# Masked blocks last in the value products, mu steps in pieces, later stores and reloads, and a fourth slab buffer in the first phase of an attention and mixture-of-experts kernel on 8 cores

## The reference, cut to what matters

```python
# per sequence x: [T=2048, C=2048]; 16 query heads of 128, 4 key/value heads
q, k, v = x @ wq, x @ wk, x @ wv;  q, k = rope(q), rope(k)
scores = q @ k.T / sqrt(128)
p_g = softmax(where(causal, scores, neg));  p_l = softmax(where(local, scores, neg))
x1 = layernorm(x + 0.5 * (p_g @ v + p_l @ v) @ wo)
# soft mixture of 16 experts with 128 slots each
x_ln = layernorm(x1) * gamma + beta
logits = l2norm(x_ln) * scale @ l2norm(mu, axis=0)      # mu: [2048, 16, 128]
dispatch = softmax(logits, axis=1);  combine = softmax(logits over all 2048 slots)
h = gelu(dispatch.T @ x_ln @ W1 + b1);  slot_out = h @ W2 + b2
out = layernorm(x1 + combine @ slot_out)
```

## Time and profile before

| what | value |
|---|---|
| three runs, us | 4929.79, 4594.17, 4884.55 (median 4884.55) |
| profiled execution, us | 4605.99 |
| its span on the slowest core (core 1), us | 4604.4 (the eight: 4560.2 to 4604.4) |
| mean granted TensorE clock, core 1 | 0.904 |
| busy share of the span | PE 77%, DVE 37%, ACT 26%, POOL 12% |
| first phase, us of the span | 0 to about 2810 |

### The profile page before, as it was taken

One profiled execution on the slowest core, in us unless ns is written; L12 is line 12 of the kernel. 1 busy time (PEld: TensorE's weight loads), 2 busy tenths in 40 slices (PEclk: granted clock), 3 DMA queues, 4 the chain that ended last, 5 costly groups with the idle time before them and its releaser, 6 DMA issues.

```text
span 4604.4 us, 66156 instructions; the slowest of 8 cores (4560.2 to 4604.4 us)
## 1 busy us (share of the span) xinstructions
PE 3542.8 (77%) x25120; PEld 2138.6 (46%) x25120; DVE 1696.5 (37%) x3526; ACT 1176.8 (26%) x1542; POOL 568.2 (12%) x1152
## 2 busy tenths in 40 slices
PE   5776676787785564575877777999979879999796
PEld 3333443544442332443544553567744335677442
DVE  2454454453442454444554443211113322111133
ACT  1122223344440111222434441221211122211111
POOL 1222122212110111111222210000000000000000
PEclk9888798999897787887999998999989989999998
DMA  9938455636527376265541133037774410467633
GB/s 186 201 104 153 102 129 106 115 115 104 110 78 131 101 142 125 88 119 117 121 100 42 47 105 129 33 124 247 243 264 183 154 72 37 144 237 248 228 137 128
DMA packets 131606, 615.71 MB, mean 134 GB/s; under 512 B 15328, under 2 KB 17376, under 8 KB 108768
## 3 DMA queue, kind: packets, MB, share of 16 engines
q1 hardware_dynamic: 106560, 430.06, 27.6%
q0 software_dynamic: 15520, 114.30, 18.8%
q10 hardware_dynamic: 9216, 67.11, 3.6%
HBM read 604.08 MB, written 188.74 MB: 172 GB/s over the span
## 4 chain that ended last, share of the span: by engine, by line
PE 53%; DMA 19%; DVE 9%; ACT 6%; issue 5%; POOL 5%; SPq 1%; another core or an unknown queue 1%; DVEq 0%; ACTq 0%; POOLq 0%
PE ob L964 10%; PE sc L882 10%; PE pr L344 7%; DMA AR<-wqkv_c 6%; PE pr L426 6%; PE ob L542 5%; DMA AR<-x1sp 3%; PE sc L509 3%; DMA out<-AR 2%; PE sc L1007 2%; ACT AR L513 2%; PE pr L372 2%; DMA AR<-wqkv_r 2%; POOL AR L525 1%; POOL AR L522 1%
## 5 line engine op out<-in xcount | busy, mean ns | idle before, releaser
L344 PE MATMUL pr<-AR 128*128 128x512 bf16 x2560 | 685.2, 406 | 202.0 <-DMA AR<-wqkv_c 103.8
L513 ACT ACTIVATE AR<-sc 128x1024 bf16<-128x1024 f32 (+2 forms) x640 | 565.6, 896 | 917.5 <-PE sc L509 908.9
L542 PE MATMUL ob<-AR 128*128 128x129 bf16 x4352 | 358.0, 231 | 320.4 <-POOL AR L529 245.6
L426 PE MATMUL pr<-AR 128*128 128x512 bf16 x2048 | 543.9, 399 | 52.7 <-DVE AR L434 30.5
L542 PEld LDWEIGHTS ob<-AR 128*128 128x128 bf16 x4352 | 298.6, 103 | 451.2 <-issue 407.1
L964 PE MATMUL ob<-AR 128*128 128x256 bf16 x4096 | 461.9, 273 | 0.0
L344 PEld LDWEIGHTS pr<-AR 128*128 128x128 bf16 x2560 | 246.8, 103 | 455.6 <-issue 276.2
L882 PE MATMUL sc<-AR 128*128 128x512 bf16 x2048 | 455.9, 381 | 0.2 <-issue 0.2
L964 PEld LDWEIGHTS ob<-AR 128*128 128x128 bf16 x4096 | 399.4, 98 | 57.5
L509 PE MATMUL sc<-AR 128*128 128x256 bf16 (+1 forms) x2304 | 350.0, 277 | 51.2 <-ACT AR L513 50.0
L509 PEld LDWEIGHTS sc<-AR 128*128 128x128 bf16 x2304 | 224.8, 102 | 180.9 <-issue 79.4
(11 more groups left out here) (97 smaller groups left out, 3910.5 us busy)
## 6 DMA issues: line engine op xcount, KB each, us to landing
AR<-w_c SPq DMA_DIRECT2D x256, 512.0 KB, 6.0
AR<-wqkv_c SPq DMA_DIRECT2D x168, 512.0 KB, 4.0
w_c<-W_r POOLq DMA_DIRECT2D x32, 2048.0 KB, 41.5
AR<-x SPq DMA_DIRECT2D x32, 1024.0 KB, 6.7
x1sp<-AR ACTq DMA_DIRECT2D x32, 1024.0 KB, 4.1
AR<-b SPq DMA_DIRECT2D x32, 1024.0 KB, 6.9
AR<-x1sp SPq DMA_DIRECT2D x32, 1024.0 KB, 5.6
out<-AR ACTq DMA_DIRECT2D x32, 1024.0 KB, 3.9
```

The source lines that it names most:

```text
L344: tm = p.pe(lambda e, b=b, c=c, w=w: e.matmul(out=pr[b], lhsT=w[:, c * 128:(c + 1) * 128], rhs=xT[:, c * 512:(c + 1) * 512], start=c == 0, ...
L426: tm = p.pe(lambda e, b=b, h=h, dg=dg, nt=nt, i=i: e.matmul(out=pr[b], lhsT=oT[i % 2][:, nt, h, :], rhs=wo[h][:, dg * 512:(dg + 1) * 512], ...
L513: ta = p.act(lambda e, b=b, eb=eb, lo=lo, hi=hi: e.activation(out=eb[:, lo:hi], in_=sc[b][:, 0:hi - lo], func=AF.Exp), tm, t_E_pe[h % 2])
L542: tm = p.pe(lambda e, q=q, o=o, j=j, eb=eb, kv=kv, last=last: e.matmul(out=ob[q][:, 0:129], lhsT=eb[:, o:o + 128], rhs=vaug[:, j, kv, 0:12 ...
```

## The change

- **Value products.** `pv(h, q)` now does only the blocks without a mask, each waiting for the chunk of exp that it reads. `pv_end(h, q)` does the masked block and the local sum. Its place for q = 0 is behind `pv(h, 1)`, for q = 1 behind the last scores of the next head. The four POOL steps become two of double size: the diagonal ones first, then the two copies. `turn` comes one head later.
- **`take_pr(hold=True)`**: an item of the projection keeps its PSUM tile, and what comes in between takes the other.
- **mu** is no generator any more: its pieces are emitted 1, 4, 5, 8, 9, 11, 15 and 20 ticks after its place; each half's sum has a PSUM tile of its own and is added on DVE. The places move to windows 1, 2, 3 and 8 to 11, each after every sixth item of the window.
- **Layer norm**: the pieces are emitted at 1, 2, 3, 13, 15, 20 and 30 ticks. `xl` lies in the lower half of the tile's own `y` buffer (two of them), so DVE's first step now waits for the store to `x1sp`, and the reload of `y` for the store to `xlnsp`.
- **Four slab buffers**, the fourth where `xlv` was; `load_slab(k + 4)`.
- **`precast`** is spread over its window; window 8 puts the eight output items of window 7 between its eight k and v items; in the other even windows k and v items stand between output items; `c_proj` is 1.5 times as large in window 15.

```diff
-        ring = [v(RING + i * 4096, BF16, 2048) for i in range(3)]
+        ring = [v(o, BF16, 2048) for o in (RING, RING + 4096, RING + 8192, XL)]
...
-        xlv = v(XL, BF16, 2048)
+        xlb = [v(Y + i * 8192, BF16, 2048) for i in range(2)]
...
+        def take_pr(hold=False):
+
+            i = 1 - prn[0]
+            if i == held[0]:
+                i = 1 - i
+            prn[0] = i
+            if hold:
+                assert held[0] is None
+                held[0] = i
             return i
...
+            def second():
+
                 tg = p.dve(lambda e: e.scalar_tensor_tensor(
-                    out=xlv, in0=y, scalar=rs[:, 1:2], in1=gamv, op0=ALU.mult, op1=ALU.mult),
-                    tx, t_gb[0], t_xl_st[0])
-                t_y_free[nt] = [tg, ts]
-                if i < 15:
-                    load_y(i + 1, nt)
+                    out=xl, in0=y, scalar=rs[:, 1:2], in1=gamv, op0=ALU.mult, op1=ALU.mult),
+                    t_norm[0], t_x1[el, n], t_gb[0])
+                tok["x"] = p.dve(lambda e: e.tensor_tensor(out=xl, in0=xl, in1=betv, op=ALU.add), tg)
...
+            for n_, fn in ((1, power), (2, bias), (3, apply), (13, second), (15, stats),
+                           (20, store), (30, reload)):
+                after(n_, fn)
...
+                    two = eb[:, jd * 256:jd * 256 + 384].rearrange("p (a c) -> p a c", a=3)[:, 0:3:2, :]
+                    tg = p.pool(lambda e, two=two: e.tensor_tensor(
+                        out=two, in0=two, in1=tri2, op=ALU.mult), ta)
                     if w > 0:
...
+                        o = (jd - 1) * 256
+                        two = eb[:, o:o + 512].rearrange("p (a c) -> p a c", a=4)[:, 0:4:3, :]
+                        tg = p.pool(lambda e, two=two, lc=loc[h % 2]: e.tensor_tensor(
+                            out=lc, in0=two, in1=tri2, op=ALU.mult), t_E_pe[h % 2])
+                    t_mask[h] = tg
...
+                for j in range(2 * w + q):
+                    o = j * 256 + 128 * q
+                    p.pe(lambda e, q=q, o=o, j=j, eb=eb, kv=kv: e.matmul(
+                        out=ob[q][:, 0:129], lhsT=eb[:, o:o + 128],
+                        rhs=vaug[:, j, kv, 0:129], start=j == 0, stop=False),
+                        t_ec[h, o // 1024], v_toks, ob_free[q], t_vone)
+
+            def pv_end(h, q):
...
                 if h > 0:
                     pv(h - 1, 1)
+                    pv_end(h - 1, 0)
                     yield c_p[1]
...
+                if h > 0:
+                    pv_end(h - 1, 1)
+                    yield 0.2
+                if h >= 4 and h % 2 == 0:
+                    turn((h - 4) // 2)
...
+            for n_, fn in ((1, lambda: square(0)), (4, lambda: add_up(0)), (5, lambda: square(1)),
+                           (8, lambda: add_up(1)), (9, root), (11, scale), (15, store),
+                           (20, more)):
+                after(n_, fn)
...
+                yield from out[0:2]
+                for n in range(2, 8):
+                    yield from out[n:n + 1]
+                    yield from kv[n - 2:n - 1]
+                yield from kv[6:]
...
+        MU_AT = {1: [0, 1, 2], 2: [3, 4], 3: [5, 6, 7], 8: [8], 9: [9, 10, 11], 10: [12, 13], 11: [14, 15]}
...
+                if pre and min(fa, fp) >= 1 - len(pre) / (len(pre_at[i]) + 0.5):
+                    precast(pre.pop(0))
```

More of the change, by code:

```diff
@@ L168, in build_program @@
               for i in range(2)]
-        loc = [[v(LOC + (i * 2 + j) * 256, BF16, 128) for j in range(2)] for i in range(2)]
+        loc = [v(LOC + i * 512, BF16, 256).rearrange("p (a c) -> p a c", a=2) for i in range(2)]
         gpv = [v(LOC + 1024 + i * 512, F32, 128) for i in range(2)]
@@ L378, in v_item @@
                     yield 1.05
[L379 to L380 removed]
+            t_ring_pe[k % 4] = tm
+            held[0] = None
+            load_slab(k + 4)
             t_xT_pe[0] = tm
@@ L422, in out_item @@
         def out_item(i, nt, dg):
-            b = take_pr()
+            b = take_pr(hold=True)
             tm = None
@@ L638, in mu_item, with square @@
         def mu_item(e_):
-            b = take_pr()
-            tm = None
-            ts = t_mu_in[e_]
-            for hf in range(2):
-                tq = p.dve(lambda e, hf=hf: e.tensor_tensor(
+            tok = {"tm": None}
+            def square(hf):
+                tok["q"] = p.dve(lambda e, hf=hf: e.tensor_tensor(
                     out=musq, in0=mus[:, hf * 1024:(hf + 1) * 1024],
-                    in1=mus[:, hf * 1024:(hf + 1) * 1024], op=ALU.mult), ts, tm)
+                    in1=mus[:, hf * 1024:(hf + 1) * 1024], op=ALU.mult), t_mu_in[e_], tok["tm"])
@@ L646, in mu_item, with add_up @@
+            def add_up(hf):
+                b = take_pr()
+                tm = None
                 for c in range(8):
-                    tm = p.pe(lambda e, b=b, c=c, hf=hf: e.matmul(
+                    tm = p.pe(lambda e, b=b, c=c: e.matmul(
                         out=pr[b][:, 0:128], lhsT=ones, rhs=musq[:, c * 128:(c + 1) * 128],
-                        start=hf == 0 and c == 0, stop=hf == 1 and c == 7),
-                        tq, pr_free[b], inc=c == 7)
-                yield 0.6
@@ L661, in mu_item @@
-            t_mu_st[0] = p.dma("sync", "D_must", d_muc[e_], mus, t)
-            t_mu_all[e_] = t_mu_st[0]
-            if e_ + 1 < NE and e_ != 3:
-                load_mu(e_ + 1)
-            yield 0.1
+                        start=c == 0, stop=c == 7), tok["q"], pr_free[b], inc=c == 7)
+                tok["tm"] = tm
+                if hf == 0:
+                    t = p.dve(lambda e, b=b: e.tensor_copy(out=muinv, in_=pr[b][:, 0:128]), tm)
+                    tok["s"] = t
+                else:
+                    t = p.dve(lambda e, b=b: e.tensor_tensor(out=muinv, in0=pr[b][:, 0:128],
+                                                             in1=muinv, op=ALU.add), tm, tok["s"])
+                    tok["s"] = t
@@ new lines, in store, with more @@
+            def store():
+                t_mu_st[0] = p.dma("sync", "D_must", d_muc[e_], mus, tok["s"])
+                t_mu_all[e_] = t_mu_st[0]
+                mu_left[0] -= 1
+            def more():
+                if e_ + 1 < NE and e_ != 7:
+                    load_mu(e_ + 1)
+            for n_, fn in ((1, lambda: square(0)), (4, lambda: add_up(0)), (5, lambda: square(1)),
+                           (8, lambda: add_up(1)), (9, root), (11, scale), (15, store),
+                           (20, more)):
+                after(n_, fn)
@@ L692, in items_of, with plain_items @@
         def items_of(i):
+            mus_ = [("m", e_) for e_ in MU_AT.get(i, [])]
+            for n, it in enumerate(plain_items(i)):
+                if mus_ and n and n % 6 == 0:
+                    yield mus_.pop(0)
+                yield it
+            assert not mus_
+        def plain_items(i):
             G = i // 2
@@ L779, in build_program @@
             n_it = len(list(items_of(i)))
-            c_proj = 4.2 * n_it
-            if i in MU_AT and MU_AT[i][0] in (0, 4):
+            c_proj = 4.2 * n_it * (1.5 if i == 15 else 1.0)
+            if i in MU_AT and MU_AT[i][0] in (0, 8):
                 load_mu(MU_AT[i][0])
-            for j in pre_at[i]:
-                precast(j)
+            pre = list(pre_at[i])
             if i == 8:
-                for it in [qk_item(4, s) for s in range(4)] + [v_item(4, kv) for kv in range(4)]:
+                first = [qk_item(4, s) for s in range(4)] + [v_item(4, kv) for kv in range(4)]
+                outs = [out_item(7, nt, dg) for nt in range(2) for dg in range(4)]
+                for it in [x for two in zip(first, outs) for x in two]:
                     for _ in it:
```

164 lines of the change are left out of this document (82 added, 82 removed).

## The result

The kernel is faster: 0.9216 of the time before (95% interval 0.9016 to 0.9415). The profiled execution took 4251.72 us where 4107 was forecast: the gain is 354 of the 499 us expected. (Executions in which one half of the chip was held at a lower clock are left out of every ratio; the highest times listed here are such ones.)

What follows compares the result with a forecast made beforehand. First phase bound by PE's queue standing still behind others. 4605.99 - 205 - 185 - 71 - 5 - 28 + 50 + 40 - 95 = 4107 us; own range 4000 to 4220 (chance 0.70), wider range 3960 to 4300.

Steps and rivals of the forecast that it cites:

- mu's squares: PE's waits at mu's sums for DVE's squares, first phase: 185 of 198.4 us gained, bounds 120 and 198.
- the DMA rival: DMA engines and DVE take back more than half of what slabs and masks give: 4315 us, chance 0.14.
- everything gained: Rival: the cover holds and the clock stays up, new waits at half price: 3910 us, chance 0.11.
- no change: Rival: masks' and mu's waits are replaced by waits of the same size: 4552 us, chance 0.03.
- slower: Rival: DVE's wait for x1sp's store becomes the first phase's clock: 5257 us, chance 0.02.
- the masks: PE's waits at the value products for POOL's masks: 205 of 245.6 us gained, 41 left, bounds 120 and 245.
- Clock: Matmuls at the low clock, first phase: less idle time gains 95 of 150 us, bounds 30 and 150.
- Denser queues: Shorter windows make DVE and ACT late more often in the first phase: 40 us added, bounds 0 and 130.
- the old stall: PE's longest wait at L575, from the old xlv store: 28 us gained, bounds 20 and 28.
- DVE's wait for x1sp: DVE newly waits for x1sp's store, some 90 us in all: 50 us added for PE, bounds 0 and 290.
- Slabs: PE's waits for weight slabs, first phase: 71 of 121.4 us gained, 50 left, bounds 20 and 115.
- Window 0: Bound by the DMA engines; the fourth buffer gains 5 of 60 us of waits, bounds 0 and 25.

Runs made afterwards that it cites:

- e10_late_musplit: Changed kernel with the layer norm's second part in single, later steps and mu's scaling in four steps; 4149.11 to 4164.20 us, ratio 0.9023 to the kernel before.
- e1: Changed kernel without DVE's addition of beta and three of four statistics steps of xl in each tile; 4153.26 to 4165.52 us, ratio 0.9014 to the kernel before.
- e6: Changed kernel with the layer norm's second part in single steps at separate ticks, same work; 4163.68 to 4175.64 us, ratio 0.9084 to the kernel before.
- e3: Changed kernel with three slab buffers and xl in a buffer of its own; 4225.53, 4229.06, 4242.25 us (one run 12573.78, unexplained), ratio 0.9179 to the kernel before.
- e2: Changed kernel with three slab buffers instead of four, nothing else different; 4273.43, 4291.14 and 4310.78 us, ratio 0.9301 to the kernel before.
- e7_burst: Changed kernel with the weight casts again in bursts at the start of each window; 4313.42, 4318.13, 4338.82 us, ratio 0.9418 to the kernel before.
- e12_changed_again: The changed kernel itself without any edit, a second series; 4235.71, 4247.08, 4248.53 and 4250.71 us, ratio 0.9221 to the kernel before.

## Why the prediction was right in direction and wrong in size

The direction and the place were right: one phase gets shorter, the waits for POOL and slabs go nearly and those for mu's squares mostly, DVE gets a new wait for x1sp, and the DMA rival (4315), everything gained (3910), no change (4552) and slower (5257) did not come true. The size was not: 4251.72 us, 145 above the 4107 and outside the forecast's own range of 4000 to 4220. By the forecast's own terms PE should have idled 877 - 205 - 185 - 71 - 5 - 28 + 50 + 40 = 473 us and lost 95 less to the clock. It idled 540, and its busy time fell by 5: 67 + 90 = 157, less the 12 us by which tail and second phase got shorter, 145.

**The step that failed: each wait was priced at what it lasts.** For the masks the 245.6 us became 16.2, better than "205 gained, 41 left". But the term took the gain in time to be the wait that goes, 205 us. Undone in the changed kernel the masks' part costs 50 us, done alone it gives 126. At the same matmul stands a second condition, `ob_free`, which the view did not show because it names the one that came last. The prediction asked whether exp would take the place; it never asked so of DVE, though `ob_free[q]` stands in the same call. What came there shows in both kernels: 55.3 us of waits for DVE before, 171.4 after, 186.1 with the masks' part alone.

**Clock: failed, 95 forecast, 5 measured** (3 as the mean of the eight cores). The granted clock rose from 0.87 to 0.90, not to the "0.93 or more" that was asked for, because slow time was cut out in which PE did nothing. The matmuls ran slow nearly as often as before. That the number of stops is what keeps them slow is tempting, and not shown: PE stopped 355 times before and 267 times after by the rows of its waits, but 267 times, too, in e10_late_musplit, where its busy time is 1811 us on the profiled core and 1844 as the mean of the eight, against 1863 and 1868.

**Denser queues: the sign right, the +40 too small.** PE's waits for DVE other than mu's squares rose by 150 us. With the terms that belong there, 50 for x1sp and -28 for the old stall, 62 were forecast, and that counts all of the 40 to DVE, though it was to hold waits for ACT too. The 88 us more are what e1 and e6 got back in part, by less in a row and by the same in smaller steps. The reason given ("60 to 70% load is more often late") was a reason of averages. The runs point to the stretch without a break, 6.3 us, against some 3 us until PE misses `ob`. Both numbers were in the prediction or before's trace.

**mu's squares: too much counted.** 185 of 198.4 were to go; 39.8 are left where "below 20" was asked for, so 159 went. Between square and sum lie three ticks, but the square itself stands in DVE's queue behind the same blocks, as at 352 us.

**DVE's wait for x1sp: right.** "Some 90 in all", 49.9 measured; worth 50 forecast, 56 to 60 by e3 against e2. Against the change the prediction held a rule of the Trainium skill (DMA: Bandwidth & Descriptors, Queues, rings and completion order: queues with work are served in turn), and read out of it that spreading the casts "only moves" the stretches in which others are slow. The trace agrees with the rule: a store is late beside a single cast too (20.3 us to landing at 1979 us, median 5.7, beside a cast issued at 1971 that landed after 24.9). It does not agree with what was read out of it: bursts give 136.5 us of such waits (e7_burst), spread casts 49.9. A cover of ten ticks takes up most of what one cast can do, and not what three do.

**Slabs: better than forecast**, 7.0 us left instead of 50 (15.1 in e12_changed_again). **Window 0**: no gain (5 forecast); PE's waits for cast slabs and xT are 38.3 and 32.3 against 39.8 and 20.5. **exp**: forecast to "rather grow", fell from 50.0 to 24.7; instead the projection waits 39.0 us for ACT's copy of `pr` (8.6 before). **Tail and second phase**: -10 and -2, within the bounds. **Window 15** took 114 us, as asked for.

In one sum: DVE's rows miss the forecast by 88 + 26 (mu) = 114. The others miss it by -25 (masks), -43 (slabs), -25 (exp, taken as unchanged), +15 (window 0) and +30 (ACT's copy), -48 in all; 114 - 48 is 66 of the 67 us by which the idle time missed.

Of the four signs by which the prediction said that it would be wrong (POOL at L581, exp over 100 us, DVE's wait for x1sp over 200, the second phase changed by over 20) none came: 16.2 us at L581, 24.7 for exp, 49.9 for x1sp, 2 us in the second phase. None of them looked at DVE and `ob`, where the miss was.

## What to carry to other kernels

Before you count a wait as gained, list every condition of the waiting instruction and ask when each of the others is met; where an in-order engine with half its time busy is one of them, expect much less than the wait: 246 us were worth 126 here with nothing else changed, and 154 were worth 50 beside the other edits. Give that engine no block longer than what its customer can bear, and cut long optional work into single steps: the same instructions in more and smaller places were worth 63 to 80 us here, against 95 for leaving half of their time out. Do not count a gain of clock from less idle time alone: 337 us of it went here, and the matmuls ran as slow as before. And when a profile puts a wait down to a step that the instruction does not wait for, look at what ended just before.
